# Second attention's keys: four products of 32 token rows in place of two zero-filled ones of 128

## The reference, cut to what matters

```python
y_dca = y[:, -DCA:, :]                # the last 16 context tokens of a sequence
y_main = y[:, :-DCA, :]               # the first 48
k_dca = _ln((y_dca @ Wkv_dca + bkv_dca)[keys])      # per head of 16 features
k     = _ln(y_main @ Wk + bk)
q     = _ln(x @ Wq + bq)
ctx   = _attn(q, k, v) + _attn(q, k_dca, v_dca)
return ctx @ Wo + bo
```

## Time and profile before

| | |
|---|---|
| median of 3 runs | 1027.32 us (1026.84 to 1027.59) |
| profiled execution, its own time | 1023.76 us |
| its span in the profile | 1021.7 us |
| instructions | 25768 |
| TensorE matmuls busy, share of the span | 870.0 us, 85% |
| VectorE, ScalarE, GpSimd busy | 66%, 42%, 33% |
| mean granted TensorE clock | 0.955 of full speed |
| steady part of the second attention, 530 to 787 us | TensorE busy 245.56 of 257.00 us |

### The profile page before, as it was taken

One profiled execution on the slowest core, in us unless ns is written; L12 is line 12 of the kernel. 1 busy time (PEld: TensorE's weight loads), 2 busy tenths in 40 slices (PEclk: granted clock), 3 DMA queues, 4 the chain that ended last, 5 costly groups with the idle time before them and its releaser, 6 DMA issues. The chain is left out here.

```text
span 1021.7 us, 25768 instructions
## 1 busy us (share of the span) xinstructions
PE 870.0 (85%) x9240; PEld 667.4 (65%) x9240; DVE 675.5 (66%) x1581; ACT 428.3 (42%) x1027; POOL 335.0 (33%) x293
## 2 busy tenths in 40 slices
PE   0799999999999899999889999999999780088883
PEld 0577777777777688989757777777776660055551
DVE  5577877778777675555367777777776479746552
ACT  1244434444344342233446556655555680023330
POOL 1443433434334040000123333333333010157763
PEclk9899999999999999999989999999999995589997
DMA  9300000000000000000001111111111089965542
GB/s 296 92 13 17 13 13 15 10 15 15 10 15 31 2 8 4 0 0 0 3 11 23 31 31 31 31 28 26 28 31 29 21 293 325 245 172 93 88 74 31
DMA packets 74907, 56.61 MB, mean 55 GB/s; under 512 B 40945, under 2 KB 70001, under 8 KB 74865
## 3 DMA queue, kind: packets, MB, share of 16 engines
q1 hardware_dynamic: 68720, 46.62, 16.2%
q0 software_dynamic: 6144, 9.44, 5.4%
HBM read 41.81 MB, written 14.22 MB: 55 GB/s over the span
## 5 line engine op out<-in xcount | busy, mean ns | idle before, releaser
L404 ACT ACTIVATE pr_t<-bank 128x512 f32<-128x512 f32 x128 | 76.4, 597 | 161.0 <-PE bank L300 160.2
L824 POOL TENSOR_TENSOR g_k_bd<-g_k_t,head_mask 128x1024 f32<-128x1024 f32 x32 | 60.6, 1895 | 134.9 <-ACT g_k_t L999 134.9
L312 PEld LDWEIGHTS bank<-v_bd,pr_t 128*64 128x64 f32 x2048 | 70.0, 137 | 26.5 <-issue 26.3
L300 PE MATMUL bank<-ident,sub 128*128 128x128 f32 x512 | 82.8, 284 | 3.6 <-ACT pr_t L404 2.8
L312 PE MATMUL bank<-v_bd,pr_t 128*64 128x18 f32 x2048 | 82.8, 214 | 0.1
L300 PEld LDWEIGHTS bank<-ident,sub 128*128 128x128 f32 x512 | 56.2, 141 | 31.3 <-issue 17.6
L481 DVE TENSOR_TENSOR sub<-bank,top 128x2048 f32<-128x2048 f32 x32 | 73.3, 2292 | 3.9 <-DVE top L477 0.2
L261 POOL TENSOR_TENSOR rot<-part_a,part_b 128x512 f32<-128x512 f32 x32 | 40.8, 1274 | 103.4 <-DVE part_b L490 103.4
L819 POOL TENSOR_TENSOR xres<-xres,g_out_bias 128x256 f32 (+1 forms) x32 | 23.4, 730 | 153.8 <-DVE g_xn L1022 153.8
L477 DVE TENSOR_REDUCE top<-bank 128x32 f32<-128x2048 f32 x32 | 73.1, 2285 | 0.9 <-PE bank L288 0.8
L648 ACT ACTIVATE f_hid<-bank,b 128x128 f32<-128x128 f32 x128 | 36.6, 368 | 85.5 <-PE bank L594 85.4
(11 more groups left out here) (204 smaller groups left out, 2063.1 us busy)
## 6 DMA issues: line engine op xcount, KB each, us to landing
e_w_gu<-in_experts_in SPq DMA_DIRECT2D x11, 768.0 KB, 10.2
table<-r_row SPq DMA_DIRECT2D x16, 320.0 KB, 9.3
e_w_d<-in_experts_out SPq DMA_DIRECT2D x11, 384.0 KB, 12.1
xres<-in_x SPq DMA_DIRECT2D x4, 1024.0 KB, 9.6
out<-xres SPq DMA_DIRECT2D x32, 128.0 KB, 1.7
xres<-in_experts_in SPq DMA_DIRECT2D x3, 768.0 KB, 21.3
keys_in<-in_ctx_t SPq DMA_DIRECT2D x32, 64.0 KB, 1.8
vals_in<-in_ctx_t SPq DMA_DIRECT2D x32, 64.0 KB, 1.8
```

Of the source, the lines that this page charges most:

```text
L300: m = pe.transpose(b_pr[:, j * P:(j + 1) * P], sub[:, v, cols], k.ident[:, :])
L312: m = pe.matmul(b_o[64 * b:64 * b + 64, hp * VW0:(hp + 1) * VW0], pr_t[:, e, j, b * S:(b + 1) * S], v_bd[:, v, b, hp, :], start=True, stop ...
L404: act.activation(pr_t[:, e, :, :].rearrange("p j q -> p (j q)"), b_pr[:, :], ACT.Exp).then_inc(a_exp, 1)
L824: pool.tensor_tensor(k_bd[:, v, :, :, :, :].rearrange("p c b h s -> p (c b) h s"), k_t[:, v, :, :].rearrange("p c (b a s) -> p (c b) a s", ...
```

## The change

`keys_in` holds each tile's context once, with the tokens ordered by kind: the 96 main tokens of the two sequences, then the 32 others. The host lays out that copy of the context (`ctx_by_kind`). The keys come from four products of 32 tokens each. Each takes all 128 rows and 32 columns of the array and writes 32 rows of the bank; nothing is added up between them. The keys' bias rows follow the new order, the two ScalarE operations that make `k_t` read the new order and write the old one, the zero-fill of `keys_in` goes, and one transfer per tile replaces two.

```diff
-        keys_in = z.sb("g_keys_in", [P, 2, 2, P])
+        keys_in = z.sb("g_keys_in", [P, 2, P])
+        rows_of_kind = (slice(0, 2 * MAIN), slice(2 * MAIN, P))
...
-            sp.wait_ge(g_fill, 2)
+            sp.wait_ge(g_fill, 1)
...
+                    sp.wait_ge(keys_done[u], 16 * i)
+                    sp.wait_ge(g_qkp, t - 1)
+                sp.dma_start(keys_in[:, u, :], ins["ctx_by_kind"][:, bass.ds(t * P, P)]).then_inc(keys_done[u], 16)
...
-            pool.memset(keys_in[:, :, :, :], 0.0).then_inc(g_fill, 1)
...
-                    pe.wait_ge(keys_done[u], 32 * (i + 1))
+                    pe.wait_ge(keys_done[u], 16 * (i + 1))
...
-                    for kind in range(2):
-                        m = pe.matmul(b_qk[:, D:2 * D], keys_in[:, u, kind, :], k.wcen[:, (2 + kind) * D:(3 + kind) * D],
-                                      start=(kind == 0), stop=(kind == 1))
+                    for kind, rows in ((0, slice(0, 32)), (0, slice(32, 64)), (0, slice(64, 2 * MAIN)), (1, rows_of_kind[1])):
+                        m = pe.matmul(b_qk[rows, D:2 * D], keys_in[:, u, rows], k.wcen[:, (2 + kind) * D:(3 + kind) * D],
+                                      start=True, stop=True)
                     m.then_inc(g_qkp, 1)
...
                     for kind, cols, _ in kinds:
-                        act.activation(k_t[:, v, :, :].rearrange("p c (b s) -> p (c b) s", b=2)[:, :, cols],
-                                       b_qk[:, D:2 * D].rearrange("p (c s) -> p c s", s=S)[:, :, cols], ACT.Identity,
+                        act.activation(k_t[:, v, :, :].rearrange("p c (b s) -> p c b s", b=2)[:, :, :, cols],
+                                       b_qk[:, D:2 * D].rearrange("p (c m) -> p c m", m=P)[:, :, rows_of_kind[kind]]
+                                       .rearrange("p c (b s) -> p c b s", b=2), ACT.Identity,
...
-            (k.wcen[b * S + first:b * S + first + count, keys], over_rows(bias, count))
-            for b in range(2) for first, count, bias in ((0, MAIN, ins["main_k_b"]), (MAIN, DCA, ins["L1_xattn_bkv_dca"][0:D]))] + [
+            (k.wcen[0:2 * MAIN, keys], over_rows(ins["main_k_b"], 2 * MAIN)),
+            (k.wcen[2 * MAIN:P, keys], over_rows(ins["L1_xattn_bkv_dca"][0:D], 2 * DCA))] + [
```

More of the change, by code:

```diff
@@ L763, in second_attention, with both @@
         kinds = ((0, slice(0, MAIN), MAIN), (1, slice(MAIN, S), DCA))
+        rows_of_kind = (slice(0, 2 * MAIN), slice(2 * MAIN, P))
         DEPTH = 5
         def sync(sp):
-            sp.wait_ge(g_fill, 2)
-            def load(dst, done, used, t, i, u):
+            sp.wait_ge(g_fill, 1)
+            def both(t, i, u):
                 if later(t, 2):
-                    sp.wait_ge(done[u], 32 * i)
-                    sp.wait_ge(used, t - 1)
+                    sp.wait_ge(keys_done[u], 16 * i)
+                    sp.wait_ge(g_qkp, t - 1)
+                sp.dma_start(keys_in[:, u, :], ins["ctx_by_kind"][:, bass.ds(t * P, P)]).then_inc(keys_done[u], 16)
+                if later(t, 2):
+                    sp.wait_ge(vals_done[u], 32 * i)
+                    sp.wait_ge(g_v, t - 1)
                 rows = ins["ctx_t"][:, bass.ds(t * P, P)].rearrange("c (b s) -> c b s", b=2)
                 for kind, cols, _ in kinds:
[L776 to L781, removed]
+                    sp.dma_start(vals_in[:, u, kind, :].rearrange("c (b s) -> c b s", b=2)[:, :, cols],
+                                 rows[:, :, cols]).then_inc(vals_done[u], 16)
             def store(t):
@@ L801, in gpsimd @@
             pool.memset(v_bd[:, :, :, :, :], 0.0).then_inc(g_fill, 1)
-            pool.wait_ge(g_fill, 4)
+            pool.wait_ge(g_fill, 3)
             for h in range(2):
@@ L810, in gpsimd @@
                         pool.tensor_scalar(ones, ones, k.kind[rows, kind:kind + 1], None, ALU.add).then_inc(g_fill, 1)
-                pool.wait_ge(g_fill, 4 + 4 * (h + 1))
+                pool.wait_ge(g_fill, 3 + 4 * (h + 1))
             pool.wait_ge(k.g_obias, 1)
@@ L949, in scalar @@
         def scalar(act):
-            act.wait_ge(g_fill, 4 + 8)
+            act.wait_ge(g_fill, 3 + 8)
             def square(tk, v):
@@ L1877, in lay_out @@
     laid["ctx_t"] = np.ascontiguousarray(a["ctx_1024"].reshape(T, C).T)
+    pairs = np.asarray(a["ctx_1024"]).reshape(NT, 2, S, C)
+    laid["ctx_by_kind"] = np.ascontiguousarray(np.concatenate(
+        [pairs[:, :, 0:MAIN].reshape(NT, 2 * MAIN, C), pairs[:, :, MAIN:S].reshape(NT, 2 * DCA, C)], axis=1).reshape(T, C).T)
     laid["pos_rows"] = np.ascontiguousarray(a["fside_BxSx2_0"].reshape(NT, P, 2).transpose(1, 0, 2))
```

## The result

The kernel after took 1013.26 us (median of 4 runs, 1010.55 to 1014.83), the kernel before 1027.09 us (4 runs beside it, 1026.84 to 1027.59). The ratio is 0.986, 95% interval 0.984 to 0.989. I had forecast 1018.4 us, with 1015 to 1024 us as the range. So it is faster, as forecast, but by 13.8 us instead of 8.9, and outside the range. The profiled executions stand nearer to the forecast: 1014.00 us after 1023.76, where I had worked out 1014.9. That nearness is partly luck, as the part on the prediction shows.

The account below looks back on a forecast made before the run. The loop through TensorE's recurring wait for `hat` was taken to set the step. 32 tiles at 0.26 us (8.4 us) plus 0.5 us for half-clock tiles gave 8.9 us: 1027.3 - 8.9 = 1018.4 us, range 1015 to 1024 us.

Parts of the forecast that it names:

- The quarters run four abreast, two slots: Keys product: the four column quarters run in parallel, two slots of 0.217 us instead of four.
- two abreast: Rival, keys product: only two quarters stream at once, four slots, 0.15 us slower per tile, 1032.1 us; chance 0.06.
- strict order: Rival, keys product: records cannot start ahead of earlier waiting ones, five slots, 0.37 us slower per tile, 1039.1 us; chance 0.05.
- A change of form costs 0.10 us going out and 0.05 coming in: TensorE, around the keys product: price of switching array tiling, included in the 0.26 us saved per tile.
- The loop through `hat` sets the step: Second attention: the loop through TensorE's recurring wait for `hat` sets the step, 4.89 + 4.04 = 8.93 us.
- `k_t`, loads and zero-fill cost nothing: `k_t`'s new reading order, the single transfer per tile and the removed zero-fill were all costed at nothing.
- 0.33 us of `k_bd` are left: Margin from the end of `k_bd` at 656.07 to the weights of `turn`, which come up to 0.25 us earlier.
- Another wait takes over: Rival: TensorE or `k_bd` sets the step, leaving only TensorE's own 0.12 us per tile, 3.8 us, 1023.5 us; chance 0.08.
- 32 tiles at 0.26 us are 8.4 us: Sum over the block: the keys end 0.26 us earlier in each of 32 tiles, 8.4 us in all.
- The 0.5 us for two tiles at half the clock: Two early keys products ran at half the clock; about double saving there adds 0.5 us, total 8.9 us.
- The profiled execution would become 1014.9 us: Whole profiled execution: 1023.76 us less the total saving of 8.9 us.
- The median of the runs is 3.56 us above it, and I take the same saving from that: Final sum: 1027.3 - 8.9 = 1018.4 us, with 1.5 us either way for changing clocks, 1015.3 to 1021.3.

Follow-up runs that it names:

- the mixed version: Kernel after with its first three keys products replaced by one over the whole array and the fourth, 32 columns, overwriting the other kind's rows: 1028.14 us, ratio 1.004.
- the third measurement: The kernel after, unchanged, measured a third time beside the kernel before, 6 runs: 1017.32 us, ratio 0.990.
- the third version: Kernel after with first values product moved ahead, wait for `k_bd` three transposes later, and keys product ahead of query product: 1005.68 us, ratio 0.982.

## Why the prediction was right, and where it was wrong

- *The quarters run four abreast, two slots.* Right: four records within 0.07 us, the set repeated takes 0.43 us. Both slower rivals, two abreast and strict order, fall with it: the keys span 0.64 us, where they need 1.08 and 1.30.
- *A change of form costs 0.10 us going out and 0.05 coming in.* Going out is right (1.06 us, and 2.11 in the mixed version). Coming in is 0.02 (second slot at 0.24 after 0.217). So the keys end 0.29 us earlier after the query product's start, and not 0.26. Of that the step keeps 0.27 (8.89 to 8.62), because the second half grew by 0.03 us, which the sum had at nothing. That 0.26 was met to the hundredth is the luck of two misses that cancel.
- *The loop through `hat` sets the step.* Right: the wait stays, the second half keeps its 4.0 us, and work saved off this loop goes mostly into the wait.
- *`k_t`, loads and zero-fill cost nothing.* Right for `k_t` and the layout: 1.000 with them and the wide products. For loads and zero-fill only the profiles say so.
- *0.33 us of `k_bd` are left.* Wrong, and without effect: the margin was counted to the end of `k_bd`, with nothing for the way from there to TensorE. Where TensorE stood waiting (the values product moved), the weights of `turn` loaded 0.41 to 0.42 us after that end; in the kernel after it is 0.51 to 0.60 us. So only 0.1 to 0.2 us were left. *Another wait takes over* did not come, but it was nearer than the prediction had it.
- *32 tiles at 0.26 us are 8.4 us.* Measured 8.5 us over the block. The 0.5 us for two tiles at half the clock were an accident of the first profile.
- *The profiled execution would become 1014.9 us.* It was 1014.00, and that it is so near is luck. Its span is 9.7 us shorter: 0.6 ahead of the block, 11.6 in the block, of which 3.1 are the two falls of the clock that this execution did not have, and behind the block it is 2.5 us longer (243.1 against 240.6 us).
- The step that failed is the last of the sum, a size and not the mechanism: "The median of the runs is 3.56 us above it, and I take the same saving from that", with "1.5 us either way" for the clock. The three shown times, 1026.84 to 1027.59, look like a kernel that repeats within 1 us. It does not: 69 runs went from 1019.97 to 1031.07, with a median of 1024.94. The 1027.09 of the result lay 2.1 us above that, and its 1013.26 lay 2.4 us below the 1015.65 of the 12 later runs of the kernel after. So of the 13.8 us some 4.5 belong to the few executions of that measurement, and 9.3 are left. Chance and a difference between chips or hours are not told apart here. From 1024.9 the same 8.9 us would have given 1016.0.

Where the scatter lies, the kept profiles show. The falls at the block's start move 3.1 us. What lies behind the block moves more: over the twelve profiles of this document it took from 239.8 to 247.9 us, in no order that follows the edits. These are the shortest (the first values product moved) and the longest (one wide product and one narrow), columns as in the earlier trace rows:

```profile
771.88:1011.68 239.80, 143.83 (x1072) 98.62 (x1064) 142.05 (x530) 76.77 (x195) 92.59 (x78) 0.85 0.57 143
```

```profile
783.05:1030.98 247.93, 148.41 (x1066) 102.79 (x1064) 141.66 (x529) 76.67 (x195) 92.19 (x77) 0.82 0.57 138
```

VectorE, ScalarE and GpSimd do the same work in both, and the longer one has the lower granted clock. Over whole executions it is the same: the four runs of the kernel after had a mean clock of 0.954 to 0.961; the six of the third measurement, 0.946 to 0.956, had a median 4.1 us higher, with the same code.

Open: over all 16 runs the difference is 9.8 us by mean and 10.5 by median, not 8.5. I make the interval of the mean difference some 8.3 to 11.3 us, by drawing anew from the runs, and some 7.4 to 10.7 with the 12 later runs alone. A straight line through all 85 runs, time against mean clock and kernel, gives 9.6 us at equal clock, 8.5 to 10.6. So 8.5 is not excluded, and a further 1 us is not either. That the shorter block shifts the falls in the last stretches to better places is not seen: behind the block the three profiles of the kernel after took 243.1 to 244.3 us, the two of the kernel before 240.6 and 242.8.

## What to carry to other kernels

On a nearly full engine, find the loop that passes through its one recurring wait, and price an edit by what it takes out of that loop. The same 0.15 us of TensorE work was worth 0.03 us per step while another loop bound, and all of it once that loop was gone. Splitting the array pays only if what it saves in slots on that loop exceeds the changes of form on it: here 0.12 us for going from the whole array to 32 columns, against 0.43 for two slots. A mixed pair of products pays the same and saves no slot. A margin that is counted to another engine's end is too large by the time until the waiting engine starts, up to 0.4 us here. And three times that agree do not give the scatter: where the profile shows the clock fall, time and profile the unchanged kernel again before an error of 1 to 2 us is put beside a forecast.

## What the runs showed of the hardware

Four products with all 128 rows and 32 columns each run abreast: eight records of 256 float32 columns in 0.64 us at 2.4 GHz from first start to last end, each next set of eight 0.43 us. Going from the whole array to 32 columns delays the next record by 0.09 us (1.06 us after the query product's start instead of 0.97), and the second record of the new form by 0.02. From the end of GpSimd's `k_bd` to the first TensorE matmul behind its wait it was 0.44 to 0.46 us where TensorE stood waiting (651.13 to 651.58); where the wait stood before the fourth transpose of a `turn`, that transpose started 0.36 to 0.37 us after `k_bd`'s end in every second step of the third version, with TensorE at work until then. In two profiles of one kernel the granted clock in the same 30 us was 0.89 and 1.00, with TensorE busy 23.15 and 22.93 us of them.
